# A vision tower on one core: new instruction orders for the attention stage, and residual products that open their PSUM banks earlier

## The reference

```python
xs = jnp.concatenate([x, *_shift4(x)], axis=-1)            # patches with four shifted copies
y = conv(xs, conv_w, stride=16) + conv_b
h = layernorm(y, 1e-3) * gamma + beta
h = h @ dense_w + dense_b
...
a1 = softmax(q1 @ k1.T / 4); a2 = softmax(q2 @ k2.T / 4)   # 8 heads of 16, in each image
o = (a1 - lam * a2) @ v
xn = group_norm(o, 4 groups over (features / 4, tokens of an image)) * gn_w + gn_b
h = layernorm(h + xn @ out_w.T + out_b)
...
g = (relu(h @ gfc1_w.T + gfc1_b) @ gfc2_w.T + gfc2_b).mean(axis=1)   # gates of an image
W1m = W1 + einsum('be,efd->bfd', g, tv_W1)                 # merged weights of each image
W2m = W2 + einsum('be,edf->bdf', g, tv_W2)
h = layernorm(h + layernorm(h + relu(h @ W1m.T + b1m) @ W2m.T + b2m) * lng + lnb)
```

## Time and profile before

| | us |
|---|---|
| median of three runs | 221.39 |
| the three runs | 217.56, 221.39, 222.84 |
| the profiled execution, whole | 218.23 |
| its span in the trace | 216.3 |
| TensorE, VectorE, ScalarE, GpSimd busy | 175.8, 132.9, 120.7, 46.7 |

### The profile page before, as it was taken

How to read it: one execution, slowest core, us unless ns; L and a number is a source line. 1 busy time by engine, 2 the same in 40 slices (tenths; PEclk the granted TensorE clock), 3 DMA queues, 4 the chain that set the end, 5 groups by cost and what they waited for, 6 DMA issues and landing times.

```text
span 216.3 us, 7966 instructions
## 1 busy us (share of the span) xinstructions
PE 175.8 (81%) x3508; PEld 123.5 (57%) x3508; DVE 132.9 (61%) x247; ACT 120.7 (56%) x223; POOL 46.7 (22%) x71
## 2 busy tenths in 40 slices
PE   0698998999979479999899999999999999990000
PEld 0233444466658455755488888888877787770000
DVE  2594136467999886752566766666664555478750
ACT  2121363486986331537856677777763444337992
POOL 2001200385096364000000000000044000018750
PEclk9999999999999855559999999999999999996555
DMA  6999996322000000000002131213100000000112
GB/s 200 381 393 386 375 274 116 86 85 82 5 6 6 3 5 3 3 0 0 0 6 80 35 83 32 83 32 83 32 6 3 3 3 6 3 3 0 37 41 73
DMA packets 9266, 16.53 MB, mean 76 GB/s; under 512 B 1598, under 2 KB 4350, under 8 KB 8720
## 3 DMA queue, kind: packets, MB, share of 16 engines
q1 hardware_dynamic: 9232, 16.02, 23.9%
HBM read 15.20 MB, written 0.82 MB: 74 GB/s over the span
## 4 chain that ended last, share of the span: by engine, by line
PE 54%; DVE 13%; ACT 12%; SPq 9%; DMA 6%; issue 4%; ACTq 0%
PE PS L1351 15%; DVE arena L376 8%; PE PS L1373 7%; SPq L397 7%; DMA cst<-consts 6%; ACT t L749 4%; PE PS L1363 4%; PE PS L1108 4%; PE PS L1168 4%; PE PS L1153 3%; PE PS L1058 3%; ACT hid L576 2%; PE PS L1187 2%; PE PS L1192 2%; PE PS L1127 2%
## 5 line engine op out<-in xcount | busy, mean ns | idle before, releaser
L376 DVE COPY arena<-PS 128x1024 f32<-128x1024 f32 x32 | 39.0, 1224 | 32.4 <-PE PS L1351 32.4
L375 ACT ACTIVATE arena<-PS 128x1024 f32<-128x1024 f32 x32 | 32.7, 1025 | 20.6 <-PE PS L1351 20.5
L1351 PE MATMUL PS<-gates,wrow 18*128 18x128 f32 x1024 | 37.2, 282 | 1.7 <-DVE arena L376 0.7
L1351 PEld LDWEIGHTS PS<-gates,wrow 18*128 18x128 f32 x1024 | 31.5, 186 | 7.9 <-DVE arena L376 5.4
L1058 PE MATMUL PS<-arena,hid 128*128 128x512 f32 (+1 forms) x64 | 27.2, 561 | 8.6 <-ACT hid L540 7.5
L1058 PEld LDWEIGHTS PS<-arena,hid 128*128 128x128 f32 x64 | 11.6, 204 | 22.1 <-issue 15.3
L519 POOL TENSOR_TENSOR t<-t,lnaff 128x2048 f32<-128x2048 f32 x1 | 4.6, 4552 | 76.1 <-PE PS L1363 76.1
L1397 PE MATMUL PS<-arena,hid 128*32 128x128 f32 x512 | 17.3, 276 | 0.0
L1373 PE MATMUL PS<-arena,t 128*32 128x128 f32 x512 | 17.3, 276 | 0.0
L1397 PEld LDWEIGHTS PS<-arena,hid 128*32 128x32 f32 x512 | 13.0, 109 | 2.7 <-issue 2.7
L714 ACT ACTIVATE hid<-hid 128x400 f32<-128x400 f32 x16 | 8.5, 537 | 10.7 <-DVE hid L985 10.7
(11 more groups left out here) (128 smaller groups left out, 294.1 us busy)
## 6 DMA issues: line engine op xcount, KB each, us to landing
arena<-windows SPq DMA_DIRECT2D x24, 256.0 KB, 8.3
wrow<-ffn_weights SPq DMA_DIRECT2D x32, 128.0 KB
hid<-conv_filter SPq DMA_DIRECT2D x8, 320.0 KB, 6.5
wrow<-ffn_weights SPq DMA_DIRECT2D x64, 8.0 KB
cst<-consts SPq DMA_DIRECT2D x1, 840.0 KB, 12.3
out<-t SPq DMA_DIRECT2D x16, 50.0 KB
cst<-consts SPq DMA_DIRECT2D x1, 322.0 KB, 9.6
arena<-windows SPq DMA_DIRECT2D x4, 64.0 KB, 8.7
```

Source lines behind the costliest of these rows:

```text
L375: return eng.activation(dst, PS[:, b:b + 2, :], ACT.Copy)
L376: return eng.tensor_copy(dst, PS[:, b:b + 2, :])
L1351: mm = pe.matmul(PS[:, merge_bank(n) + r, :].rearrange("p (b k j) -> p k b j", k=4, j=NJ)[:, k], wrow[32 * r:32 * r + KR, w], gates[32 * r ...
```

## The change

It does three things. It rewrites the order of the calls on TensorE, ScalarE and VectorE between the first conv steps and the gates. It moves each `residual(q)` ahead of the group products of its bank: the residual opens the bank (`start=True`), and `group_mean` and `group_var` write with `start=False` into their columns. And it changes what these wait for: `residual` no longer waits for `gln_done`, the first half of the group root of its quarter, but for the score shifts that read the bank (7 for quarter 2, else 8), or, for quarter 3, for `x2_ready`, the first quarter's normalisation. `group_mean` no longer waits for these. No instruction is added or taken away. GpSimd and SyncE are unchanged.

```diff
@@ scalar
             y_rstd(0)
+            h_evac(0)
             y_square(1)
-            h_evac(0)
-            y_rstd(1)
             query_evac(0)
             keys_evac(0, 1)
+            y_rstd(1)
             lambda_exp()
...
             soft_exp(3)
+            keys_evac(3, 1)
             keys_evac(3, 0)
-            keys_evac(3, 1)
...
@@ tensor
             def group_mean(q):
                 pe.wait_ge(gsum_done, q + 1)
-                pe.wait_ge(shifted, NU8)
+                pe.matmul(spare(q, 0), C("gnsum"), gns[:, 0, q * QI:(q + 1) * QI], start=False, stop=True, skip_group_check=True).then_inc(gmean_done, 1)
+
+            def group_var(q):
+                pe.wait_ge(gsqsum_done, q + 1)
+                pe.matmul(spare(q, 1), C("gnsum"), gns[:, 1, q * QI:(q + 1) * QI], start=False, stop=True, skip_group_check=True).then_inc(gvar_done, 1)
+
+            def residual(q):
+
                 if q == 3:
                     pe.wait_ge(x2_ready, 1)
-                pe.matmul(spare(q, 0), C("gnsum"), gns[:, 0, q * QI:(q + 1) * QI], start=True, stop=True).then_inc(gmean_done, 1)
-
-            def group_var(q):
-                pe.wait_ge(gsqsum_done, q + 1)
-                pe.matmul(spare(q, 1), C("gnsum"), gns[:, 1, q * QI:(q + 1) * QI], start=True, stop=True).then_inc(gvar_done, 1)
-
-            def residual(q):
-
-                pe.wait_ge(gln_done, q + 1)
-                pe.matmul(PS[:, out_bank[q], 0:QT], cmat[:, :], t2[:, cols(q)], start=True, stop=False)
+                else:
+                    pe.wait_ge(shifted, NU8 - 1 if q == 2 else NU8)
+                pe.matmul(PS[:, out_bank[q], 0:QT], cmat[:, :], t2[:, cols(q)], start=True, stop=False, skip_group_check=True)
...
             conv(0, 0)
-            conv(0, 1)
             conv(1, 0)
             conv(1, 1)
+            conv(0, 1)
...
+            dense(0)
             conv(1, 7)
-            dense(0)
-            y_var(1)
...
             v_proj(0)
-            scores(6)
             v_proj(1)
             v_proj(2)
             v_proj(3)
-            scores(7)
+            scores(6)
             values(0)
             values(1)
+            scores(7)
             values(2)
+            values(3)
+            residual(0)
             group_mean(0)
-            values(3)
+            residual(1)
+            residual(2)
             group_var(0)
+            group_mean(1)
             values(4)
-            residual(0)
             values(5)
             out_proj(0)
-            group_mean(1)
+            group_var(1)
+            group_mean(2)
             r_var(0)
...
```

More of the change, by code:

```diff
@@ L651, in _ @@
             soft_exp(1)
+            y_square(3)
             keys_evac(2, 0)
-            y_square(3)
             y_rstd(3)
@@ L920, in _ @@
             soft_shift(2)
+            y_scale(3)
             query_evac(1, 2)
-            y_scale(3)
             prob_transpose(0)
             soft_shift(3)
-            small_evac()
-            soft_sum(2)
-            query_evac(0, 3)
-            query_evac(1, 3)
-            soft_sum(3)
-            soft_shift(4)
+            query_evac(0, 3)
+            soft_sum(2)
+            soft_sum(3)
+            query_evac(1, 3)
+            soft_shift(4)
+            small_evac()
             soft_shift(5)
             soft_sum(4)
+            prob_transpose(1)
+            soft_sum(5)
             soft_shift(6)
-            soft_sum(5)
-            prob_transpose(1)
-            soft_shift(7)
             o_sum(0)
             o_sum(1)
+            soft_shift(7)
             group_sum(0)
+            o_sum(2)
             soft_sum(6)
             group_centre(0)
+            o_sum(3)
+            group_sum(1)
+            group_square_sum(0)
             prob_transpose(2)
-            group_square_sum(0)
-            o_sum(2)
             soft_sum(7)
-            o_sum(3)
+            group_centre(1)
             group_scale(0)
-            group_sum(1)
+            group_square_sum(1)
             o_sum(4)
@@ L1249, in _ @@
             conv(2, 1)
+            y_var(1)
+            scores(0)
             conv(2, 2)
-            scores(0)
             conv(2, 3)
```

72 lines of the change are left out of this document (33 added, 39 removed).

## The result

| | before | after |
|---|---|---|
| median of four runs, side by side | 219.47 | 221.14 |
| the four runs | 217.46 to 222.84 | 220.26 to 223.24 |
| the profiled execution, whole | 218.23 | 223.24 |
| its span | 216.3 | 221.5 |

The ratio after to before is 1.0185, with a 95% interval of 1.0123 to 1.0247: no gain, and the median of 221.14 is just above the range of 212.5 to 221.0. The runs of each kernel fall into two groups some 4 us apart, the upper one with a lower mean granted clock, and the ratio leaves the upper group of before out (its two faster runs, 217.5, stand in it), while all four runs of after were upper ones. The medians of the table, with both groups in, are 1.7 us apart. What makes the groups is the subject of the first two experiments.

A forecast was written before the change was run, and what follows sets the result against it. VectorE was taken to bound 57 to 80 us, then TensorE at half clock. Gains along the queues and the clock's return at 93 sum to 3.0 to 4.2, taken 3.5: 220.0 - 3.5 = 216.5 us, range 212.5 to 221.0.

The forecast's parts named there:

- Start, gain 0.9 us: To 41 us: reordered convs, dense(0), evacuations and keys let proj(1,0) start at 40.5, not 41.4.
- VectorE's full stretch, to 79.2: From 59.6 us, 19.6 us of VectorE work without holes; soft_sum(7) ends near 79.2 (80.43 before), softmax gain 1.3 us.
- this asks that nothing in front of it is late: Condition for VectorE's full stretch: scores(6) ends at 66.6, wanted 67.5; step 6's exponential ends at 70.4, wanted 73.3.
- They cost nothing: Three residual products behind values(3), 3 x 0.75 us at full clock, free since group_var(0) waits until 76.5.
- TensorE's lead of 3.2 us at values(7): TensorE's queue at half clock, 80 to 92 us: values(7) ends at 86.75 against 89.98.
- The clock's return at 93: Full TensorE clock back between 90.5 and 95.5 us, taken 93, after a run of 400-column products from 87.2.
- Sum to the first merge, 3.0 to 4.2: Total gain up to the first merge, 3.0 to 4.2 us, taken 3.5; first merge near 105.5.
- The rest the same length as now: Behind the gates, merge loops from the first merge on keep instructions, waits and length; no gain or loss.
- Rival 3: Clock stays down into the merges, deciding if not back by about 101 us: slower, taken 222.8 us; chance 0.12.
- Rival 1: Clock returns late, or a queue (scores(6), keys (3,1)) holds another up: 217.5 to 219, taken 218.2 us; chance 0.25.
- Rival 2: TensorE's clock does not fall near 74 us, or only later and briefly: 214.2 us; chance 0.13.

The follow-up runs named there:

- the first two experiments: Changed kernel timed again unedited, 219.45 us (before beside it 219.31); then six clock-keeping products ahead of merges 2 to 4, in the changed kernel 217.26, in before 218.47.
- the 20 tiny products: Changed kernel plus twenty 32-column products ahead of conv(1,2), to shift the borders of code blocks; one execution, 225.09 us.
- v_proj in 16 products: Changed kernel with six clock-keeping products in the merges, v_proj making values in 16 products, not 64 (values not the reference's): 217.55 us.
- the second profile: Profile of an upper run of the changed kernel, timed again with no edit; median of its 12 runs 219.45 us.
- the residual rule: Before plus only each residual opening its bank right ahead of its own group_mean, spread out: 214.87 us with six clock-keeping products in the merges, 218.27 without.
- residual(2) put back: Changed kernel with six clock-keeping products in the merges, residual(2) moved from ahead of group_var(0) to right behind out_proj(0): 216.03 us.
- with the clock held: Kernel plus six unread 128x128 products, two ahead of each of merge pieces 2 to 4: before 218.47 us (219.64 in another set), changed kernel 217.26.
- The six products: Unread 128x128 products, two ahead of each of merge pieces 2 to 4: added to the changed kernel 217.26 us, to before 218.47.

## Why the prediction was wrong, point by point

- **Start, gain 0.9 us.** Right in the profile: proj(1,0) at 40.42, forecast 40.5. y_rstd(3) came at 51.89 (51.8), h_evac(3) at 54.84 (54.6), scores(4) at 58.12 (57.75), scores(5) at 60.48 (60.05), the second softmax sum of the pair ended at 59.40 (59.2), the keys at 63.01 (62.6): within 0.5 us each.
- **VectorE's full stretch, to 79.2.** It held to 70.5 and then broke; soft_sum(7) ended at 81.98, 1.5 later than before. The condition that failed is "this asks that nothing in front of it is late". The trace of before had the code-loading wait, 1.30 us, and I read it as part of what brought the clock down, not as something fixed to the count of instructions. The new order put it behind the second instruction of the last scores, which VectorE wants at once; before it stood in the value steps, which it wants later.
- **"They cost nothing", of the three residuals.** residual(0) stands ahead of group_mean(0), for which VectorE waited 1.49 us. I had priced the fall of the clock into group_var(0), not into the mean in front of it.
- **TensorE's lead of 3.2 us at values(7).** It was 0.4 (89.55 against 89.98): what stands above took the rest.
- **The clock's return at 93.** 95.8, outside 90.5 to 95.5 by a little. The reason I gave, a run of big products at 87.2, was right in kind, but I didn't see that the same rule speaks against the change: three such products spent at 75 to 79 brought back full clock only for 78.7 to 82.1, in the kernels with the 20 tiny products and with v_proj in 16 products not at all, and were missing at 80 to 90. That 95.8 is so near is partly luck: the same order gave 92.0 to 95.8 from profile to profile.
- **Sum to the first merge, 3.0 to 4.2.** 2.0 us. x2_scale(3) ended at 103.22, later than the 100.8 to 101.9 forecast; from there the gates took 3.91 us (forecast 4.2).
- **"The rest the same length as now."** This is the step that failed most, a term that the sum put at nothing: 6.0 us lost in the opening merges of the profiled execution, 4.5 in the second profile. The instructions and waits there are the same, as I said, but the clock isn't. The four runs of the changed kernel that kept the clock there, by their mean clock, took 214.94 to 216.52, the forecast being 216.5; the others took 219.26 and more. Rival 3 had the place (1.2 us in each of the first three merges, 3.6 in all), but another mechanism: the clock was back at 95.8, well ahead of its border of 101, and fell again. I had listed "falls again" only in the gates, and had the spread of the three runs, 5.3 us, before me without asking what differed between them.
- Rival 1 was right about a queue that holds another up, with another queue (the last scores, and not the sixth step's or the keys). Rival 2's late fall did not come: 71.9, sooner than 74.0.

What is **shown**: code loading as the two "issue" waits of the changed kernel; the clock in the merges as its loss; and that the place of the big products moves the clock's return. With the residual rule it came at 84.9, 86.5 and 83.8 in three kernels, without it at 94.4 to 97.9 in four profiles of the old order; with residual(2) put back, at 88.0 against 92.0 to 95.8. Each is one profile. Idle time doesn't explain it: in before TensorE had none over 0.2 us from 85.8 us on, and the clock came back only at 97.9. What the earlier return is worth at the end is shown for the residual rule (214.87 against 218.47, the first merge at 103.19 against 107.39), not for residual(2). What is **open**: why the clock falls in the merges at all, why in 12 of 16 runs of the changed kernel, and whether more often than in before (43 of 80), which these counts can't settle; what made the short recovery near 80, which came in four of six profiles with the three residuals together; and whether the start's 0.9 us reach the end. No kernel moved a code border away from the last scores and nothing else, so the share of that wait in the 1.2 us short of the forecast at the gates isn't measured by itself.

The fastest kernels are the residual rule in before with the clock held, 214.87, and with the start as well, 214.81, against 219.3 to 221.6 for before in the three sets. Against before's lower group that is 1.1% (ratio 0.989) and 1.3% (0.9868, 0.9797 to 0.9939).

## What to carry to other kernels

- Before you count on a stage "that isn't touched", look at what differs between the runs of the kernel: two groups of times with two mean clocks say that some stage has a clock that can go either way, and a few cheap products there may be worth more than the order you are working on.
- In this kernel the lowered clock came back sooner where big products followed each other than where small ones stood between them. Try such an order first, and don't spend the big products where something is waited for.
- A TensorE "issue" wait that stays at the same count of instructions is code loading. A change of order slides it along the work; see that it doesn't land in front of what the fullest engine waits for.
- A median where you expected it is not yet the mechanism. Two kernels here had the expected time while the first merge, which was to carry the gain, did not move.

## What the runs showed of the hardware that was not expected

- A code border cost TensorE 1.3 to 1.6 us in a burst of small products (1.62, 1.43, and 1.59, 1.33 where it was moved). "Issue" waits of the same kind, at 69 to 78 us, in the other profiles are 0.4 to 2.2 us long (0.38 and 2.18 with residual(2) put back); for these the cause is read from their place, not tested. A border ahead of 400-column products, or in value steps at half clock, cost nothing that shows (the packets at 75.0 and 88.5 us of after).
- A busy TensorE isn't enough for full clock: it was busy 5.00 of 5.00 us at 0.50 in the stretch 79 to 84 of before, and the fall at 112.5 us of after shows in a half-microsecond window in which it was fully busy. In the kernel with v_proj in 16 products it was busy 19.92 of 20 us at 0.50, from 75 to 95. The rows don't say what the chip counts. The Trainium skill ("TensorE: Matmul & The Clock Gate", section "HAM oscillation — how this bites in real kernels") puts such falls down to idle gaps. Its example is a kernel that idles for a transfer between bursts, for longer than either of the gaps of 0.45 and 0.26 us ahead of this fall. Before had the same two gaps and its profile kept the clock, so here idle gaps alone don't tell the one from the other. The six products fill the second gap and leave the first, and the clock stayed up.
- The same program loses the clock in a stage in some executions and not in others: 214.94 to 216.52 us and 219.26 to 221.21 us for the changed kernel. The fall was seen in both profiles of it that were taken, both upper runs; the lower runs were not profiled.
